# Segment sums of two graph layers: 24-bit messages as two 12-bit parts in one product of 256 columns, and half of the one-hot tiles on GpSimd

## The chip, the cores and the metric

The kernel runs on 1 core of one Trainium2 chip. The metric is the device time of one execution in microseconds (us); the time of a kernel is the median of its runs.

## The reference

Four graph layers run one after the other over 3125 nodes with 128 features, and 103125 edges (50000 random pairs in both directions and one loop per node), sorted by target. Layers 0 (attention) and 1 (softmax gathering) are not touched. The change is in layers 2 and 3. Cut to what matters:

```
# layer 2
h = concat([x[row], x[col], edge_attr]) @ W1 + b1
h = relu((h - mean) * rsqrt(var + 1e-5) * gamma + beta)     # mean, var over all edges
sums = segment_sum(h @ W2 + b2, row); counts = segment_sum(1, row)
out = x + sums / (counts + 1)
# layer 3
m = relu(concat([x[src], type_emb[edge_type]]) @ msg_W.T + msg_b)
agg = segment_sum(m, dst) / max(deg, 1)
out = layernorm(x + agg @ upd_W.T + upd_b) * g + b
```

The kernel applies the node products before the edges are formed, and W2 after the sums, so that the work per edge is: add the rows of two nodes (or of a node and a type), ReLU, add into the row of one node.

## The kernel before

Nodes lie in 25 blocks of 128 (NB = 25, KT = 50). The edges have been sorted into buckets, so that a tile of 128 edges has its sources in one block and its targets in one block. Rows are picked and summed by products with one-hot matrices. The five engines are programmed by hand: each runs its own list in order and waits on semaphores. DVE is VectorE, ACT ScalarE, PE TensorE, POOL GpSimd, SP the queue that issues the transfers.

**Layer 2** (`pe_b2_main`, `dve_b2_main`, and the loop over `main_groups()` in `act_buckets`): 325 groups of up to 4 tiles, 1225 tiles. A pass over one source block k has 13 groups and 49 tiles: a unit of 7 groups (six of 4 tiles, the last of 2) and a unit of 6 groups (five of 4, the last of 3). For each tile PE does seven bf16 products of 128 columns into a PSUM bank (lines 3472, 3474, 3476; "H" below). ACT takes the ReLU of the group's bank into `msgs` (line 3413). Then PE adds the tile into the sums of its node block by one f32 product, with the one-hot tile `col_hot` as weights and the message, with a column of ones for the count, as 129 moving columns (line 3496; "A" below). DVE makes `col_hot`, one instruction a tile (line 3279). In the last pass, k = 24, half of the tiles belong to other blocks: their product goes into bank 4 or 5 in turn (line 3493), and DVE adds the bank into `S2` and `counts` (lines 3292, 3293), before PE may use that bank again two such products later.

**Layer 3** (`pe_b3`, `dve_b3`): 319 groups, 1225 tiles. Each of the first 24 node blocks has 50 tiles in 13 groups: 7 groups of 4, then 5 of 4 and one of 2; the last block has 25 tiles in 7 groups. H is four bf16 products a tile (lines 3518, 3520), ReLU is line 3428, the one-hot tile line 3349, A is one f32 product of 128 columns (line 3533).

**Row-hots.** The weights of H are the one-hot rows of a whole unit (6 or 7 groups) in two buffers. They come by transfer as numbers, and DVE turns them into one-hots with two long instructions a unit: `dve_unit_hot` (lines 3173, 3174), placed behind the col_hots of the unit's fifth group, for the unit that follows; `dve_unit_hot3` (lines 3325, 3326) behind those of the last group but one. PE can't begin the next unit's first H without them.

**Order of PE.** H(n), A(n-1), H(n+1), A(n), ... H(n) needs the ReLU of group n-4 (four banks). DVE makes the col_hots of group n as soon as A(n-2) is done (two buffers); nothing in DVE's list waits for ACT.

Of the kernel before, what the change touches and what calls it, by code (L numbers as in the profile page):

```python
# [7 lines left out]
F32 = mybir.dt.float32  # L8
I32 = mybir.dt.int32
# [5 lines left out]
P = 128  # L15
# [285 lines left out]
class BucketSignals:  # L301


    def __init__(self, g):
# [56 lines left out]
        self.d_pair_count = self.d_window  # L361
        self.drawn_pe = self.pre_pe
# [20 lines left out]
def program(nc, a, out):  # L383
    ctx = ExitStack()
    with ctx:
# [86 lines left out]

        arena_c = sb("arena_c", [P, C_WORDS])
# [199 lines left out]
        msgs = [words(C_, 12100 + s * 516, [P, 4, D + 1]) for s in range(2)]  # L673
        col_hot = [words(C_, 13132 + s * 512, [P, 4, P]) for s in range(2)]
# [2531 lines left out]
        def dve_b2_stats(e, own):  # L3206
# [51 lines left out]
            for s in range(2):  # L3258
                e.memset(msgs[s][:, :, D:D + 1], 1.0)
# [8 lines left out]

        def dve_b2_main(e, own):
            all_groups = main_groups()  # L3270
            counts = stat[:, 2, :]
            extras = 0
            for at in range(GROUPS + 2):
                if at < GROUPS:
                    u, k, bs = all_groups[at]
                    if at >= 2:
                        e.wait_ge(sig.added_pe, at - 1)
                    for i, (b, j) in enumerate(pair_tiles(bs)):
                        hot = e.tensor_scalar(col_hot[at % 2][:, i, :], iota_row, src_lo[:, b, 2 * k + j:2 * k + j + 1], None, ALU.is_equal)  # L3279
                    hot.then_inc(sig.col_hot, 1)  # L3280
                    if at == pairs_before(u) + 4 and u + 1 < 2 * NB:
                        dve_unit_hot(e, u + 1)
                if at >= 2:
                    u, k, bs = all_groups[at - 2]
                    if k == NB - 1:
                        for b in bs:
                            if b < NB - 1:
# [4 lines left out]
                                e.tensor_tensor(S2[:, b, :], S2[:, b, :], ps[:, 0:D], ALU.add)  # L3292
                                e.tensor_tensor(counts[:, b:b + 1], counts[:, b:b + 1], ps[:, D:D + 1], ALU.add).then_inc(sig.extra_dve, 1)
                    if at - 2 == (k + 1) * NPAIR - 1:
                        ps = bank[6 + k % 2]
                        e.wait_ge(sig.added_pe, at - 1)
                        e.tensor_copy(counts[:, k:k + 1], ps[:, D:D + 1])
                        e.tensor_copy(S2[:, k, :], ps[:, 0:D]).then_inc(sig.block_dve, 1)
# [29 lines left out]
        def dve_b3(e, own):  # L3328
# [13 lines left out]
            for u in range(2 * NB + 1):  # L3342
                if u < 2 * NB:
                    b = u // 2
                    for i, ts in enumerate(unit3_tiles(u)):
                        if at >= 2:
                            e.wait_ge(sig.added3_pe, at - 1)
                        for i_, t in enumerate(ts):
                            hot = e.tensor_scalar(col_hot[at % 2][:, i_, :], iota_row, dst_lo[:, b, t:t + 1], None, ALU.is_equal)  # L3349
# [4 lines left out]
                        if i == 2 and u % 2 == 0 and u:  # L3354
                            dve_b3_block(e, b - 1)
            dve_b3_block(e, NB - 1)
# [40 lines left out]
        def act_buckets(e):  # L3397
# [274 lines left out]
```

## Time and profile before

| | before |
|---|---|
| median of 3 runs | 4507.58 us (4504.23 to 4513.55) |
| the profiled execution's own time | 4506.15 us |
| its span, first to last instruction | 4504.0 us |
| granted TensorE clock, mean over the span | 0.896 |
| busy share: PE, PE weight load, DVE, ACT, POOL | 79%, 69%, 71%, 48%, 21% |
| main loop of layer 2 | 3037.4 to 3812.4 us |
| main loop of layer 3 | 3883.5 to 4450.8 us |

Between the span and the time of the same execution lie 2.15 us. POOL's 21% lies wholly in the first half of the span; in the two loops it does nothing. A matmul's duration in the rows holds the time until its result is written, so rows overlap: the pace of PE is read from one start to the next. A f32 product stands as two records.

### The profile page before, as it was taken

How to read it: one execution, taken by the hardware profiler on the slowest of the kernel's cores; microseconds unless marked ns; L12 is line 12 of the kernel's file. 1: busy time of each engine (PE TensorE's matmuls, PEld its weight loads, DVE VectorE, ACT ScalarE, POOL GpSimd, SP SyncE). 2: the span in 40 equal slices, each digit the busy share in tenths (PEclk: the TensorE clock that was granted, in tenths of full speed). 3: DMA queues.
4: the chain of work that ended last, by engine and by line, in shares of the span. 5: the costliest groups of instructions: out<-in, count | busy, mean ns of one | idle time of the engine just before them, and what ended most of it. 6: DMA issues, size and time to landing. Idle time of an engine off the chain costs nothing.

```text
span 4504.0 us, 93109 instructions
## 1 busy us (share of the span) xinstructions
PE 3567.1 (79%) x35307; PEld 3108.5 (69%) x35307; DVE 3209.6 (71%) x7198; ACT 2176.5 (48%) x6143; POOL 964.7 (21%) x1005
## 2 busy tenths in 40 slices
PE   1488899889999451666648888669999999699996
PEld 1266666666666331666647887449999998699995
DVE  5589888878898446999868787674444445666666
ACT  2366666667777223788747667212222222333332
POOL 0466577757677400000000000000000000000000
PEclk7799998999999675878779999889999999899998
DMA  5666676767777301000011011333334432233322
GB/s 110 200 186 184 172 205 197 195 171 211 209 214 211 90 5 39 10 12 12 9 35 46 38 45 45 106 109 104 113 109 116 116 109 77 63 102 102 98 97 65
DMA packets 418314, 488.81 MB, mean 109 GB/s; under 512 B 178078, under 2 KB 329924, under 8 KB 417725
## 3 DMA queue, kind: packets, MB, share of 16 engines
q1 hardware_dynamic: 358861, 305.18, 23.7%
q0 software_dynamic: 58992, 177.50, 13.7%
q8 instruction: 288, 4.72, 0.4%
q14 instruction: 173, 1.42, 0.1%
HBM read 376.80 MB, written 105.72 MB: 107 GB/s over the span
## 4 chain that ended last, share of the span: by engine, by line
PE 62%; DVE 22%; ACT 5%; issue 4%; DMA 3%; SPq 2%; POOL 1%; DVEq 0%; POOLq 0%; ACTq 0%
PE bank L3533 6%; PE bank L3496 6%; PE bank L3520 5%; PE bank L3474 5%; PE bank L3476 5%; PE bank L2325 4%; PE bank L2331 3%; PE bank L2336 3%; PE bank L3442 2%; PE bank L2898 2%; PE bank L2316 2%; ACT arena_c L2861 2%; PE bank L2389 2%; PE bank L2307 2%; DVE arena_b L1749 2%
## 5 line engine op out<-in xcount | busy, mean ns | idle before, releaser
L1112 POOL DMA_INDIRECT arena_a<-src_table,src_tix x808 | 775.9, 960 | 353.1 <-issue 228.3
L3279 DVE TENSOR_SCALAR arena_c<-arena_c 128x128 f32<-128x128 f32 x1225 | 268.9, 281 | 402.4 <-PE bank L3496 402.4
L3413 ACT ACTIVATE arena_c<-bank 128x512 f32<-128x512 f32 (+2 forms) x325 | 186.5, 574 | 591.2 <-PE bank L3476 591.2
L2898 PE MATMUL bank<-arena_a,arena_c 128*128 128x150 f32 x1800 | 289.3, 331 | 173.4 <-ACT arena_c L2864 173.4
L3349 DVE TENSOR_SCALAR arena_c<-arena_c 128x128 f32<-128x128 f32 x1225 | 265.7, 280 | 203.6 <-PE bank L3533 203.6
L3474 PE MATMUL bank<-arena_c,arena_a 128*128 128x128 bf16 x3675 | 406.2, 219 | 0.0
L3476 PE MATMUL bank<-arena_c,arena_a 128*128 128x128 bf16 x3675 | 406.2, 219 | 0.0
L2898 PEld LDWEIGHTS bank<-arena_a,arena_c 128*128 128x128 f32 x1800 | 283.7, 225 | 176.5 <-ACT arena_c L2864 176.5
L3428 ACT ACTIVATE arena_c<-bank 128x512 f32<-128x512 f32 (+1 forms) x319 | 185.2, 581 | 386.8 <-PE bank L3520 386.8
L3533 PE MATMUL bank<-arena_c 128*128 128x128 f32 x2450 | 343.1, 282 | 0.0
L3496 PE MATMUL bank<-arena_c 128*128 128x129 f32 x2402 | 338.6, 281 | 0.0
L3520 PE MATMUL bank<-arena_c,arena_a 128*128 128x128 bf16 x3675 | 309.3, 220 | 0.0
L2861 ACT ACTIVATE arena_c<-arena_c,arena_b 128x128 f32<-128x128 f32 x900 | 265.7, 387 | 89.9 <-DVE arena_b L2778 89.9
L2331 PEld LDWEIGHTS bank<-arena_b 128*128 128x128 f32 x1616 | 224.4, 201 | 111.1 <-issue 107.5
L3533 PEld LDWEIGHTS bank<-arena_c 128*128 128x128 f32 x2450 | 299.4, 192 | 0.0
L3472 PE MATMUL bank<-src_tix,arena_a 128*128 128x128 bf16 x1225 | 268.8, 219 | 34.5 <-DVE arena_c L3156 34.5
L3496 PEld LDWEIGHTS bank<-arena_c 128*128 128x128 f32 x2402 | 294.2, 191 | 0.0
L1300 ACT ACTIVATE arena_a<-arena_a 128x128 f32<-128x128 f32 x808 | 239.3, 297 | 95.7 <-DVE arena_a L1769 88.2
L3518 PE MATMUL bank<-src_tix,arena_a 128*128 128x128 bf16 x1225 | 269.2, 220 | 15.8 <-DVE arena_a L3326 15.8
L3474 PEld LDWEIGHTS bank<-arena_c,arena_a 128*128 128x128 bf16 x3675 | 257.5, 98 | 4.0
L3520 PEld LDWEIGHTS bank<-arena_c,arena_a 128*128 128x128 bf16 x3675 | 257.8, 98 | 3.5
L3476 PEld LDWEIGHTS bank<-arena_c,arena_a 128*128 128x128 bf16 x3675 | 257.6, 98 | 0.0
(583 smaller groups left out, 9263.7 us busy)
## 6 DMA issues: line engine op xcount, KB each, us to landing
y_rows<-arena_c SPq DMA_DIRECT2D x101, 576.0 KB
arena_a<-bucket_rows SPq DMA_DIRECT2D x50, 832.0 KB
arena_a<-bucket_rows SPq DMA_DIRECT2D x50, 768.0 KB
arena_a<-bucket_lists SPq DMA_DIRECT2D x25, 896.0 KB, 4.6
pair_counts<-arena_c SPq DMA_DIRECT2D x25, 800.0 KB
arena_a<-bucket_lists SPq DMA_DIRECT2D x25, 704.0 KB, 4.4
arena_a<-src_table,src_tix POOLq DMA_INDIRECT x808
arena_c<-edge_attr SPq DMA_DIRECT2D x100, 128.0 KB
```

Source lines behind the costliest of these rows:

```text
L1112: e.indirect_dma_start(out_, None, table, bass.IndirectOffsetOnAxis(ap=idx, axis=0)).then_inc(sem, 16)
L2331: q_ = e.matmul(bank[1][:, t * P:(t + 1) * P], pick[s][:, 4 * hf + t, :], win[r][:, 0:D], start=True, stop=True)
L2861: away = e.activation(hot_pos[s][:, j, :], iota_row, ACT.Abs, bias=minus_pos[s][:, j:j + 1])
L2898: put = e.matmul(bank[2 + s][:, 0:3 * KT], hot_pos[s][:, j, :], routed_v[s][:, j, :, :].rearrange("p f k -> p (f k)"), start=(j == 0), sto ...
L3279: hot = e.tensor_scalar(col_hot[at % 2][:, i, :], iota_row, src_lo[:, b, 2 * k + j:2 * k + j + 1], None, ALU.is_equal)
L3472: e.matmul(to, attr_rows[s][:, c_], Wc12, start=True, stop=False)
L3474: e.matmul(to, row_hot[0][s][:, c_], A3[:, part, sb_ * D:(sb_ + 1) * D], start=False, stop=False)
L3476: put = e.matmul(to, row_hot[1][s][:, c_], B3[:, part, b * D:(b + 1) * D], start=False, stop=(part == 2))
L3496: put = e.matmul(bank[6 + k % 2][:, 0:D + 1], col_hot[at % 2][:, i, :], msgs[at % 2][:, i, :], start=(first and i == into_k[0]), stop=(las ...
L3518: e.matmul(to, row_hot[1][s][:, c_], E48, start=True, stop=False)
L3520: put = e.matmul(to, row_hot[0][s][:, c_], A3[:, part, k * D:(k + 1) * D], start=False, stop=(part == 2))
L3533: put = e.matmul(bank[6 + b % 2][:, 0:D], col_hot[at % 2][:, i_, :], msgs[at % 2][:, i_, 0:D], start=(first and i_ == 0), stop=(last and i ...
```

## The change

In both loops the message is made in two parts of 12 bits, in a format that PE takes as float32r: ACT writes the high part, max(x, 0) rounded, and DVE writes the low part, max(x, 0) minus the high part, with a new instruction a group that reads the PSUM bank (`dve_low_parts`). A multiplies the one-hot tile, float32r too, with both parts side by side, 256 columns a tile, and the two halves of the sum are added when a block is done (one reduction instead of a copy in layer 2; one more instruction in layer 3). Counts are no longer summed by PE: they are taken once from `node_sums`. Messages and one-hots have three buffers (RING_M = 3) instead of two. GpSimd makes the one-hots of a group's third and fourth tile (`pool_b2_main`, `pool_b3`), DVE those of the first and second. PE's order becomes H(n), A(n-2). H(n) now waits for the low part of group n-4.

```diff
+        msg_parts = part_buffers("msg_parts", base_b, 0, RING_M, [P, 2, 4, D])
+        msg_parts3 = part_buffers("msg_parts3", base_c, 7304, RING_M, [P, 2, 4, D])
+        node_hot = part_buffers("node_hot", base_a, 10752, RING_M, [P, 4, P])
...
+        def dve_low_parts(e, at, nt, high_made, low_made, parts):
+            e.wait_ge(high_made, at + 1)
+            to = parts[at % RING_M]
+            e.scalar_tensor_tensor(out=to[:, 1, 0:nt, :], in0=bank[at % 4][:, 0:nt * P].rearrange("p (t f) -> p t f", f=P), scalar=0.0,
+                                   in1=to[:, 0, 0:nt, :], op0=ALU.max, op1=ALU.subtract).then_inc(low_made, 1)
...
+        def pool_b2_main(e):
+            for at, (u, k, bs) in enumerate(main_groups()):
+                nt = len(pair_tiles(bs))
+                if nt > 2:
+                    if at >= RING_M:
+                        e.wait_ge(sig.added_pe, at - RING_M + 1)
+                    for i in range(2, nt):
+                        hot = source_hot(e, at, i)
+                    hot.then_inc(sig.col_hot_pool, 1)
...
         def dve_b2_main(e, own):
-            for at in range(GROUPS + 2):
+            for at in range(GROUPS + 3):
                 if at < GROUPS:
                     u, k, bs = all_groups[at]
-                    if at >= 2:
-                        e.wait_ge(sig.added_pe, at - 1)
-                    for i, (b, j) in enumerate(pair_tiles(bs)):
-                        hot = e.tensor_scalar(col_hot[at % 2][:, i, :], iota_row, src_lo[...], None, ALU.is_equal)
+                    dve_low_parts(e, at, nt, sig.relu, sig.low, msg_parts)
+                    if at >= RING_M:
+                        e.wait_ge(sig.added_pe, at - RING_M + 1)
+                    for i in range(min(nt, 2)):
+                        hot = source_hot(e, at, i)
                     hot.then_inc(sig.col_hot, 1)
                     if at == pairs_before(u) + 4 and u + 1 < 2 * NB:
                         dve_unit_hot(e, u + 1)
-                if at >= 2:
-                    u, k, bs = all_groups[at - 2]
+                if at >= 3:
+                    u, k, bs = all_groups[at - 3]
...
-                                e.tensor_tensor(S2[:, b, :], S2[:, b, :], ps[:, 0:D], ALU.add)
-                                e.tensor_tensor(counts[:, b:b + 1], counts[:, b:b + 1], ps[:, D:D + 1], ALU.add).then_inc(sig.extra_dve, 1)
+                                own.step(e.tensor_tensor(S2[:, b, :], S2[:, b, :], ps[:, 0:D], ALU.add))
+                                e.tensor_tensor(S2[:, b, :], S2[:, b, :], ps[:, D:2 * D], ALU.add).then_inc(sig.extra_dve, 1)
...
         def pe_b2_main(e):
-            for n in range(GROUPS + 1):
+            for n in range(GROUPS + 2):
...
-                        e.wait_ge(sig.relu, n - 3)
+                        e.wait_ge(sig.low, NB + n - 3)
...
-                if n >= 1:
-                    at = n - 1
+                if n >= 2:
+                    at = n - 2
...
-                        put = e.matmul(bank[6 + k % 2][:, 0:D + 1], col_hot[at % 2][:, i, :], msgs[at % 2][:, i, :],
+                        put = e.matmul(bank[6 + k % 2][:, 0:2 * D], hots[:, i, :], parts[:, :, i, :],
```

Layer 3 is changed in the same way (`dve_b3`, `pe_b3`, `pool_b3`). Three places in the lists of the engines:

DVE in layer 3, around the row-hots that are made in an odd unit, before (line 3349 the col_hots, 24 being six groups, 3325 and 3326 the row-hots of the next unit, 3362 the end of a block):

```order
L3349 TENSOR_SCALAR arena_c<-arena_c 128x128 x24
L3325 TENSOR_SCALAR arena_a<-arena_a,arena_c 48x3584
L3326 TENSOR_SCALAR arena_a<-arena_a,node_id 128x3584
L3349 TENSOR_SCALAR arena_c<-arena_c 128x128 x14
L3362 TENSOR_SCALAR arena_b<-bank6,stat 128x128
```

and the same place now (bank numbers kept; line 3328 the low part, 3023 the one-hots, 3386 and 3387 the row-hots):

```order
L3328 SCALAR_TENSOR_TENSOR msg_parts32_54<-bank2,msg_parts32_54 128x512
L3023 TENSOR_SCALAR node_hot2_57<-arena_c 128x128 x2
L3328 SCALAR_TENSOR_TENSOR msg_parts30_52<-bank3,msg_parts30_52 128x512
L3023 TENSOR_SCALAR node_hot0_55<-arena_c 128x128 x2
L3386 TENSOR_SCALAR arena_a<-arena_a,arena_c 48x3584
L3387 TENSOR_SCALAR arena_a<-arena_a,node_id 128x3584
L3328 SCALAR_TENSOR_TENSOR msg_parts31_53<-bank0,msg_parts31_53 128x256
```

The row-hots stand behind the same group as before, but that group now begins with an instruction that reads its bank after H and the ReLU.

DVE in the last pass of layer 2, before (line 3279 the col_hots of group n, 3292 and 3293 the additions for group n-2):

```order
L3279 TENSOR_SCALAR arena_c<-arena_c 128x128 x4
L3292 TENSOR_TENSOR arena_b<-arena_b,bank4 128x128
L3293 TENSOR_TENSOR stat<-stat,bank4 128x1
L3292 TENSOR_TENSOR arena_b<-arena_b,bank5 128x128
L3293 TENSOR_TENSOR stat<-stat,bank5 128x1
```

and now (3328 and 3310 the low part and one-hots of group n, 3355 and 3356 the additions for group n-3):

```order
L3328 SCALAR_TENSOR_TENSOR msg_parts0_49<-bank3,msg_parts0_49 128x512
L3310 TENSOR_SCALAR node_hot0_55<-arena_c 128x128 x2
L3355 TENSOR_TENSOR arena_b<-arena_b,bank4 128x128
L3356 TENSOR_TENSOR arena_b<-arena_b,bank4 128x128
L3355 TENSOR_TENSOR arena_b<-arena_b,bank5 128x128
L3356 TENSOR_TENSOR arena_b<-arena_b,bank5 128x128
```

The additions that free banks 4 and 5 now stand behind a low part as well.

PE in the last pass of layer 2, now: the last tile of H(n) (lines 3536, 3538, 3540), then A(n-2), whose first two products (3561) need the banks that those additions free, then H(n+1):

```order
L3536 MATMUL bank3<-src_tix,arena_a 128x128
L3538 MATMUL bank3<-arena_c,arena_a 128x128 x3
L3540 MATMUL bank3<-arena_c,arena_a 128x128 x3
L3561 MATMUL bank4<-msg_parts1_50,node_hot1_56 128x256
L3561 MATMUL bank5<-msg_parts1_50,node_hot1_56 128x256
L3564 MATMUL bank6<-msg_parts1_50,node_hot1_56 128x256 x2
L3536 MATMUL bank0<-src_tix,arena_a 128x128
```

Before, A(n-1) stood there, with the same four products of 129 columns.

## Rows read from the trace of the kernel before

**Rows 1.** The two loops: length, busy (xcount) PE, PEld, DVE, ACT, POOL, clock, DMA.

```profile
3037.40:3812.40 775.00, 773.20 (x11025) 768.68 (x11025) 371.83 (x1419) 186.45 (x325) 0.00 (x0) 1.00 0.38 108
3883.50:4450.80 567.30, 567.26 (x7350) 562.58 (x7350) 361.88 (x1347) 185.24 (x319) 0.00 (x0) 1.00 0.30 97
```

**Rows 2.** Timeline of a group of layer 2: start, length, instructions merged, idle before.

```profile
3400.56 1.11 PE L3496 MATMUL bank<-arena_c 128*128 128x129 f32 x8
3400.76 0.60 ACT L3413 ACTIVATE arena_c<-bank 128x512 f32<-128x512 f32 x1 [1.92 <-PE bank L3476]
3401.51 0.22 PE L3472 MATMUL bank<-src_tix,arena_a 128*128 128x128 bf16 x1
...
3401.71 0.87 DVE L3279 TENSOR_SCALAR arena_c<-arena_c 128x128 f32<-128x128 f32 x4 [1.64 <-PE bank L3496]
```

**Rows 3.** Timeline of layer 3 around two pairs of row-hots, DVE.

```profile
4113.62 1.14 DVE L3325 TENSOR_SCALAR arena_a<-arena_a,arena_c 48x3584 bf16<-48x3584 bf16 x1
4114.69 1.14 DVE L3326 TENSOR_SCALAR arena_a<-arena_a,node_id 128x3584 bf16<-128x3584 bf16 x1
...
4126.50 0.94 DVE L3326 TENSOR_SCALAR arena_a<-arena_a,node_id 128x2816 bf16<-128x2816 bf16 x1
...
4136.68 1.14 DVE L3325 TENSOR_SCALAR arena_a<-arena_a,arena_c 48x3584 bf16<-48x3584 bf16 x1
```

**Rows 4.** The same stretch, PE: the first H behind those row-hots.

```profile
4115.88 0.23 PE L3518 MATMUL bank<-src_tix,arena_a 128*128 128x128 bf16 x1
```

**Rows 5.** Timeline of layer 2, DVE: the first of a pair of row-hots.

```profile
3312.56 1.08 DVE L3173 TENSOR_SCALAR arena_a<-arena_a,node_id 128x3328 bf16<-128x3328 bf16 x1
```

**Rows 6.** Timeline of layer 2's last pass, PE and DVE.

```profile
3805.80 0.66 PE L3493 MATMUL bank<-arena_c 128*128 128x129 f32 x4
...
3807.73 0.28 DVE L3292 TENSOR_TENSOR arena_b<-arena_b,bank 128x128 f32<-128x128 f32 x1
...
3808.31 0.66 PE L3493 MATMUL bank<-arena_c 128*128 128x129 f32 x4
```

**Rows 7.** Groups of instructions: count | busy us, mean ns | idle before.

```profile
L3474 PE MATMUL bank<-arena_c,arena_a 128*128 128x128 bf16 x3675 | 406.2, 219 | 0.0
L3442 PE MATMUL bank<-arena_c,arena_a 128*128 128x384 bf16 x325 | 56.8, 334 | 13.5 <-DVE arena_c L3156 13.5
L3037 DVE SCALAR_TENSOR_TENSOR arena_c<-arena_c 128x512 f32<-128x512 f32 x150 | 102.7, 685 | 47.2 <-ACT arena_c L3082 47.0
L1087 POOL TENSOR_SCALAR_AFFINE_SELECT ident<-ident 128x128 f32<-128x128 f32 x1 | 0.3, 290 | 1.5 <-DVE edge_ok L1565 1.5
L1112 POOL DMA_INDIRECT arena_a<-src_table,src_tix x808 | 775.9, 960 | 353.1 <-issue 228.3 <-DVE arena_c L1757 124.8
```

**Rows 8.** One line's instructions: durations in ns, min/median/max, first and last start.

```profile
L1717 DVE TENSOR_SCALAR arena_b<-arena_b,node_id x25: 277/280/493, 540.8 to 857.1; 128x128 f32<-128x128 f32 x25
```

**Rows 9.** Layer 1: waits of PE on L3014, two stretches (us, times, longest).

```profile
PE bank L3114 <- DVE arena_b L3014: 3.4, 3, 1.1
PE bank L3114 <- DVE Hn L3014: 2.2, 2, 1.1
...
PE bank L3114 <- DVE Hn L3014: 5.6, 5, 1.1
PE bank L3114 <- DVE arena_b L3014: 5.6, 5, 1.1
```

**Rows 10.** Busy time and clock of those two stretches, and slices behind one wait.

```profile
2350.00:2450.00 100.00, 83.01 (x1313) 78.59 (x1311) 84.75 (x163) 74.50 (x222) 0.00 (x0) 1.00 0.11 43
2500.00:2700.00 200.00, 168.12 (x2475) 159.80 (x2474) 159.24 (x307) 138.72 (x408) 0.00 (x0) 0.92 0.11 43
...
2512.00:2513.00 1.00, 0.24 (x5) 0.24 (x6) 1.00 (x2) 0.00 (x0) 0.00 (x0) 0.93 1.01 422
2513.00:2514.00 1.00, 1.00 (x19) 1.00 (x17) 0.90 (x6) 0.00 (x0) 0.00 (x0) 0.50 0.55 218
...
2516.00:2517.00 1.00, 1.00 (x16) 0.99 (x16) 0.73 (x3) 0.76 (x4) 0.00 (x0) 0.86 0.00 0
```

More of the change, by code:

```diff
@@ L8 @@
 F32 = mybir.dt.float32
+F32R = mybir.dt.float32r
 I32 = mybir.dt.int32
@@ L361, in __init__ @@
         self.d_pair_count = self.d_window
+        self.low = self.routed
+        self.low3 = self.weighed
+        self.col_hot_pool = self.spread
+        self.col_hot3_pool = self.away
         self.drawn_pe = self.pre_pe
@@ L446, in program @@
         RING = 4
+        base_a = nc.sbuf_base
         arena_a = sb("arena_a", [P, RING * TPB * 3 * D])
+        base_b = nc.sbuf_base
         arena_b = sb("arena_b", [P, 2 * NB * D])
@@ L3000, in pool_buckets, with target_hot, pool_b3 @@
             e.wait_ge(g.nodes_ready, 4)
+            pool_b2_main(e)
+            pool_b3(e)
+        def target_hot(e, at, i, b, t):
+            return e.tensor_scalar(node_hot[at % RING_M][:, i, :], iota_row, dst_lo[:, b, t:t + 1], None, ALU.is_equal)
+        def pool_b3(e):
+            e.wait_ge(sig.split_dve, 8)
+            at = 0
+            for u in range(2 * NB):
+                for ts in unit3_tiles(u):
+                    if len(ts) > 2:
+                        if at >= RING_M:
+                            e.wait_ge(sig.added3_pe, at - RING_M + 1)
+                        for i in range(2, len(ts)):
+                            hot = target_hot(e, at, i, u // 2, ts[i])
+                        hot.then_inc(sig.col_hot3_pool, 1)
+                    at += 1
         def dve_b_hot(e, b, i):
@@ L3257, in dve_b2_stats @@
             dve_wc_parts(e, own)
-            for s in range(2):
-                e.memset(msgs[s][:, :, D:D + 1], 1.0)
+            own.step(e.tensor_copy(stat[:, 2, :], node_sums[:, 0:NB, 2]))
             dve_split(e, scaled_tables, 2)
@@ L3345, in dve_b3 @@
                     for i, ts in enumerate(unit3_tiles(u)):
[L3346 to L3349, printed above, removed]
+                        dve_low_parts(e, at, len(ts), sig.relu3, sig.low3, msg_parts3)
+                        if at >= RING_M:
+                            e.wait_ge(sig.added3_pe, at - RING_M + 1)
+                        for i_, t in enumerate(ts[0:2]):
+                            hot = target_hot(e, at, i_, b, t)
                         hot.then_inc(sig.col_hot3, 1)
@@ L3353, in dve_b3, with dve_b3_block @@
                             dve_unit_hot3(e, u + 1)
-                        if i == 2 and u % 2 == 0 and u:
-                            dve_b3_block(e, b - 1)
-            dve_b3_block(e, NB - 1)
+                        if i == 3 and u % 2 == 0 and u:
+                            dve_b3_block(e, own, b - 1)
+            dve_b3_block(e, own, NB - 1)
             e.wait_ge(sig.block3_dve, NB)
             e.drain().then_inc(g.nodes_ready, 1)
-        def dve_b3_block(e, b):
+        def dve_b3_block(e, own, b):
             e.wait_ge(sig.added3_pe, groups3_before(2 * b + 2))
-            e.tensor_scalar(S1[:, b, :], bank[6 + b % 2][:, 0:D], stat[:, 0, b:b + 1], None, ALU.mult).then_inc(sig.block3_dve, 1)
+            own.step(e.tensor_reduce(S1[:, b, :], bank[6 + b % 2][:, 0:2 * D].rearrange("p (a f) -> p f a", a=2), AX, ALU.add))
+            e.tensor_scalar(S1[:, b, :], S1[:, b, :], stat[:, 0, b:b + 1], None, ALU.mult).then_inc(sig.block3_dve, 1)
         def dve_split_y(e):
@@ L3504, in pe_b3 @@
             flat = [(u, i, ts) for u in range(2 * NB) for i, ts in enumerate(unit3_tiles(u))]
-            for n in range(len(flat) + 1):
+            by_pool = 0
+            for n in range(len(flat) + 2):
                 if n < len(flat):
```

60 lines of the change are left out of this document (37 added, 23 removed).

## The prediction

> **What bounds the kernel now.** I read the busy time of the two loops first, then the timeline of one group, then the places where DVE does its long instructions. In both loops PE is busy to within 2 us of 775.0 and of 567.3 us at the full clock, while DVE is busy 371.8 and 361.9, ACT 186 and 185, and POOL does nothing [rows 1]. Whatever is saved of PE there is saved of the whole, as long as nobody makes PE wait. In a group of layer 2, A takes from 3400.56 to the next H at 3401.51, 0.95 us for 8 records, so 0.118 a record and 0.236 a tile [rows 2]; a whole group is 3808.31 - 3805.80 = 2.51 us [rows 6], which leaves 1.56 for the 28 products of H, 0.056 each. A pass of layer 2 is 49 x (7 x 0.056 + 0.236) = 30.8 us, and 25 of them make 770 of the 775. In layer 3 a block lasts 4136.68 - 4113.62 = 23.06 us [rows 3], and 50 x (4 x 0.056 + 0.236) = 23.0. So both loops go at PE's pace.
>
> How far DVE runs ahead is what the reader should see next. Its col_hots start at 3401.71, when A has ended, in the middle of H(n) [rows 2]: they don't wait for H or ReLU. Even so, in layer 3 the second row-hot ends at 4114.69 + 1.14 = 4115.83 [rows 3], and PE begins the next unit's H at 4115.88 [rows 4]. That cover is used up to the last 0.05 us.
>
> **The change, part by part.** *A.* No float32r product is in the trace. From below, 256 more columns at bf16's pace: (334 - 219) / 256 = 0.45 ns a column [rows 7], 0.115 us a tile; from above, f32's pace for 256 columns, 0.47. One record's pace, 0.118, is what a weight load and 256 columns at 0.45 ns take side by side, and I take it: half of the 0.236 before. For its page on number formats (the Trainium skill, "FP8 and Floating Point Precision", TensorE Precision Notes: true fp32 takes four passes) one pass of twice the columns would be half too. If nothing waits, a pass becomes 49 x 0.51 = 25.0 and a block 50 x 0.342 = 17.1 us: 25 x 5.8 + 24.5 x 5.9 = 290 us off.
>
> *DVE.* The low part is new: a two-operand instruction of 512 columns takes 0.685 us [rows 7], and I let the next start 0.61 behind it (rows overlap by 0.07: 1.14 long, 1.07 apart, [rows 3]). Two one-hots are 0.39 ((0.87 - 0.28) / 3 = 0.197 apart, [rows 2]). So 1.0 us a group for 0.8 before, with the row-hots 17 us a block in layer 3: DVE's total fits under PE. Its order doesn't. The row-hots now stand behind a low part that waits for H and ReLU. From the end of H's issue, at time 0: ReLU 0.20 to 0.80 (3400.56 to 3400.76, 0.60 long, [rows 2]), low part 0.84, one-hots 1.45, row-hots from 1.85. In layer 3's odd units they end at 1.85 + 1.07 + 1.14 = 4.06, and PE may begin at 4.10. It has until then only A(n-2) 0.47, the H of 2 tiles 0.45 and another A 0.47: 1.39. **It stands 2.7 us.** In even units (0.94 long, [rows 3]): 1.85 + 0.87 + 0.94 + 0.05 = 3.7 against 0.47 + 0.90 + 0.47 = 1.84: **1.9 us.** Layer 2's odd units (1.08 long, [rows 5]): 1.85 + 1.01 + 1.08 + 0.05 = 4.0 against 0.47 + 1.17 + 0.47 = 2.1: **1.9 us**; its even units have one more group in between, 3.8, and stand 0.1.
>
> *GpSimd.* Nothing of this form is in the trace. Its 128x128 select took 0.29 us, the longest common instruction 0.96 [rows 7]; I take 0.35, near the select, so 0.7 a group, under every period. They begin when A is done. One pair falls between A(n-2) and DVE's one-hots and meets nothing; the pair behind A(n-1) falls into the row-hots. A DVE instruction of the one-hots' form took 0.277 at its shortest, but 0.493 once while POOL was at work [rows 8]. So I add one POOL instruction, 0.35, to each pair of row-hots. The bounds are 0 (they never meet) and about 1.0 (both get in between, at 0.5 each); 0.96 for one is the far end. The Trainium skill ("SBUF — State Buffer", Who interferes with whom) says that a two-port DVE instruction and a GpSimd one exclude each other for their whole length, whichever came first. By that rule 0.35 or 0.7 is right; the stretched row above agrees with it but doesn't prove it.
>
> *Last pass of layer 2.* Banks 4 and 5 are freed by additions that now wait for the low part of the group whose H has just ended. After the two one-hots at 1.85: an addition 0.28 [rows 6] and, behind a semaphore, a second; bank 4 is free at 2.5, bank 5 at 3.0. PE then does A's last three products, 0.36, and H, 1.56: 4.9 us a group instead of 2.5. Ten such groups, the short ones (3 and 4 us), the first (2.0) and a pair of row-hots (1.9) make 60 us for 30.8.
>
> *Clock.* In layer 1 PE waits 1.1 us on L3014: five times between 2350 and 2450, with the clock at full, and ten times between 2500 and 2700, with a mean clock of 0.92 [rows 9, 10]. The slices behind one wait show it: 0.93, three at 0.50, then 0.86, which is 1.7 us lost [rows 10]; ten of these are the 0.08 x 200 = 16 us missing. So 10 of 15 waits of 1.1 us had a fall to 1.2 GHz behind them. PE was not densely at work around those, and here it is, so for waits of 2.2 us I take a fall after 6 in 10, for 3.1 us after 8 in 10 (bounds none and all), each 1.7 us. In the last pass PE works 2.0 of 4.9 us; at the lower level a group would be H 3.1, the chain 2.9 and the last three products 0.7, so 6.7; I take 75 us for the pass (bounds 60, 80).
>
> *Sum.* Layer 2, 24 passes: 25.0 + 1.9 + 0.1 + 2 x 0.35 = 27.6, and 1.0 for the clock: 28.6 for 30.8, 24 x 2.2 = **-53**. Last pass 75 - 31 = **+44**. Layer 3: 17.1 + 1.9 + 2.7 + 0.7 = 22.4, and 1.4 falls, 2.4: 24.8 for 23.06, 24 x 1.7 = **+41**. The ends of the loops, where a low part now lies between the last ReLU and the last A: **+2**. Together +34 on 4506.15, the profiled execution's time, which lies 1.4 us under the median: **4540 us**. The counts, their column and the memsets cost and give nothing: they lay beside PE. The reduction per block lies on DVE behind A's that it has already waited for, and costs nothing while DVE keeps 0.3 us a group; without that, 0.7 a block.
>
> **The rivals.** *The clock stays up.* The standing times remain, the falls don't: 24 x (27.6 - 30.8) = -77, last pass +29, layer 3 24 x (22.4 - 23.06) = -17, ends +2: 4443 us, faster. It decides the sign; the ten waits with falls speak against it, the five without for it. *No collision between POOL and DVE*, with falls: 0.7 off each pass and block: 4506, no change. *POOL is dearer* (0.5 us or more, or both its instructions get in between): another 0.7 a pass and block and a few more falls: 4585; at 0.96 each layer 3 would be bound by POOL at 24 x 0.96 = 23.0 a block before any wait, some 4620. *PE never waits*, because the row-hots are ready after all: 4216; the order of DVE's list speaks against it. *float32r goes at f32's pace*: 0.47 a tile adds 0.23 x 2450, over 5000 us.
>
> **How the numbers follow.** Forecast 0.40, clock up 0.22, no collision 0.13, POOL dearer 0.15, PE never waits 0.05, f32's pace 0.03, other 0.02. The range 4440 to 4605 takes in the first four. 0.2% (9 us) is about what a measurement of this kernel can tell from no change. Faster by more: 0.22 + 0.05 + 0.05 of "no collision" + 0.04 of the forecast's lower edge = 0.36; within: 0.08; slower: 0.56. The forecast's own range is 4500 to 4580.
>
> **What the profile would show.** A: records of 128x256, 0.118 apart. DVE's low part at 0.68, behind ReLU. PE idle before the first H of a unit, put down to the row-hots, once a pass in layer 2 and twice a block in layer 3, 1.9 to 3 us: some 65 us in layer 2 and 125 in layer 3. In the last pass ten waits on the additions, 2.5 us each and more. POOL's one-hots at 0.35, and row-hots up to 0.35 longer or later than 1.14. The granted clock 0.9 in layer 3 instead of 1.00, half to two thirds in the last pass. Most likely to be wrong: the number of falls, and POOL's price.

## The result, and the profile after

The changed kernel takes **4491.89 us** (median of 20 runs) and the kernel before 4508.16 (median of 20). The ratio is 0.9964, with a 95% interval of 0.9954 to 0.9974: 0.36% faster, where 0.7% slower was forecast. One of the changed kernel's runs, at 4855.59 us and a mean clock of 0.71 instead of 0.88, is left out of the comparison. The profiled execution took 4497.49 us.

The first part of the page, of the changed kernel:

```profile
PE 3385.2 (75%) x32857; PEld 2891.7 (64%) x32857; DVE 3410.4 (76%) x6679; ACT 2176.8 (48%) x6143; POOL 1770.1 (39%) x2167
```

Busy time and clock of the 24 passes of layer 2, its last pass, and the loop of layer 3, in the columns of [rows 1]:

```profile
3045.90:3713.00 667.10, 629.73 (x9470) 612.23 (x9471) 444.30 (x1058) 180.14 (x314) 359.35 (x557) 1.00 0.44 125
3713.00:3780.40 67.40, 42.43 (x334) 37.40 (x331) 26.39 (x86) 6.32 (x12) 11.19 (x19) 0.62 0.02 5
3852.40:4441.90 589.50, 489.07 (x6125) 466.23 (x6125) 462.88 (x1103) 185.27 (x319) 438.24 (x587) 0.92 0.29 93
```

Layer 2 goes from 775.0 to 734.5 us (-40.5) and layer 3 from 567.3 to 589.5 (+22.2) [rows 1]. Between the loops lie 72.0 us instead of 71.1. The loop of layer 2 begins 8.5 us later than before, though ahead of it only a copy of the counts stands in place of the memsets, and PE's wait just ahead of the loop is 34.5 us in both; in the experiments, whose code up to there is the same, it begins between 3036 and 3051, so this is the spread of a single execution. PE is no longer busy throughout: 94% in the first stretch, 63% and 83% in the others.

PE's waits in the two loops (us in total, times, longest):

```profile
PE bank L3587 <- DVE arena_a L3387: 115.7, 50, 15.9
PE bank L3536 <- DVE arena_a L3211: 37.4, 24, 1.6
...
PE bank L3561 <- DVE arena_b L3356: 24.8, 10, 4.3
```

The first two are the waits for the row-hots (3387 in layer 3, where the longest one is the wait ahead of the loop, and 3211 in layer 2), the third is that for the additions in the last pass. They stand where the prediction put them.

A unit's end in layer 2 (timeline; it answers to [rows 2, 5]):

```profile
3401.44 0.72 PE L3564 MATMUL bank<-msg_parts,node_hot 128*128 128x256 f32 x4
3401.67 0.60 ACT L3476 ACTIVATE msg_parts<-bank 128x512 fp32r<-128x512 f32 x1 [1.50 <-PE bank L3540]
3402.00 0.23 PE L3536 MATMUL bank<-src_tix,arena_a 128*128 128x128 bf16 x1
...
3402.30 0.69 DVE L3328 SCALAR_TENSOR_TENSOR msg_parts<-bank,msg_parts 128x512 fp32r<-128x512 f32 x1 [0.89 <-ACT msg_parts L3476]
...
3402.91 0.47 DVE L3310 TENSOR_SCALAR node_hot<-arena_c 128x128 fp32r<-128x128 f32 x2
...
3403.30 1.08 DVE L3210 TENSOR_SCALAR arena_a<-arena_a,node_id 128x3328 bf16<-128x3328 bf16 x1
...
3403.97 2.45 POOL L3310 TENSOR_SCALAR node_hot<-arena_c 128x128 fp32r<-128x128 f32 x2 [1.11 <-PE bank L3564]
3404.29 1.08 DVE L3211 TENSOR_SCALAR arena_a<-arena_a,node_id 128x3328 bf16<-128x3328 bf16 x1
...
3405.43 0.23 PE L3536 MATMUL bank<-src_tix,arena_a 128*128 128x128 bf16 x1 [1.56 <-DVE arena_a L3211]
...
3432.99 0.23 PE L3536 MATMUL bank<-src_tix,arena_a 128*128 128x128 bf16 x1 [1.56 <-DVE arena_a L3211]
```

H's issue ends at 3401.44, where A begins; then come ReLU, low part, one-hots, two row-hots, and the next unit's H at 3405.43. These are 3.99 us, 4.0 in the prediction. The row-hots are 1.08 long, as before, and nothing lies between them. The same wait comes back 27.56 us later: that is a pass (30.8 before). Four products of A take 3402.00 - 3401.44 = 0.56 us, 0.14 a tile. From H's issue to the next PE has 0.56 + 1.16 (three tiles of H) + 0.56 = 2.3 us of work, so it stands 1.7; the profile, which counts idle time from the end of the last record, has 1.56.

The same place in layer 3 (timeline), and the clock around it (two windows):

```profile
4110.83 0.72 PE L3605 MATMUL bank<-msg_parts,node_hot 128*128 128x256 f32 x4
...
4112.62 2.65 POOL L3023 TENSOR_SCALAR node_hot<-arena_c 128x128 fp32r<-128x128 f32 x1 [1.24 <-PE bank L3605]
...
4112.68 1.14 DVE L3386 TENSOR_SCALAR arena_a<-arena_a,arena_c 48x3584 bf16<-48x3584 bf16 x1
4113.74 1.14 DVE L3387 TENSOR_SCALAR arena_a<-arena_a,node_id 128x3584 bf16<-128x3584 bf16 x1
...
4114.94 0.23 PE L3587 MATMUL bank<-src_tix,arena_a 128*128 128x128 bf16 x1 [2.41 <-DVE arena_a L3387]
...
4128.16 0.23 PE L3587 MATMUL bank<-src_tix,arena_a 128*128 128x128 bf16 x1 [1.66 <-DVE arena_a L3387]
...
4138.89 0.23 PE L3587 MATMUL bank<-src_tix,arena_a 128*128 128x128 bf16 x1 [2.41 <-DVE arena_a L3387]
```

```profile
4114.90:4118.90 4.00, 3.96 (x37) 3.87 (x37) 1.81 (x6) 0.60 (x1) 2.31 (x4) 0.57 0.25 80
4118.90:4136.00 17.10, 15.44 (x215) 14.81 (x213) 14.23 (x35) 6.59 (x12) 13.34 (x20) 1.00 0.23 75
```

From the end of H's issue (4110.83) to the next H (4114.94) are 4.11 us. A block is 4138.89 - 4114.94 = 23.95 us (23.06 before). It holds a wait of 2.41 us, one of 1.66, and one fall to the lower level, behind the longer wait: 4.00 us at 0.57, so 1.7 us lost. Slices of 1 us over the whole loop show 24 such falls, one behind each wait of 2.41 us, and a low clock at the loop's start and end: 44 us lost in all, which is the 0.92 of the loop.

### The profile page after: what moved, and what is told of

Its sections match the earlier page's. It is cut to its first block, busy times and chain, and to the rows that moved or that the text cites. A ratio compares the mean times of both kernels' runs of the same rounds, so it can differ in the third digit from the quotient of the medians.

```text
span 4495.7 us, 88908 instructions
## 1 busy us (share of the span) xinstructions
PE 3385.2 (75%) x32857; PEld 2891.7 (64%) x32857; DVE 3410.4 (76%) x6679; ACT 2176.8 (48%) x6143; POOL 1770.1 (39%) x2167
## 4 chain that ended last, share of the span: by engine, by line
PE 55%; DVE 27%; ACT 7%; issue 4%; DMA 3%; SPq 2%; POOL 1%; DVEq 0%; POOLq 0%; ACTq 0%
PE bank L3589 5%; PE bank L3540 4%; PE bank L3538 4%; PE bank L2342 4%; PE bank L2348 3%; PE bank L2353 3%; PE bank L3564 3%; PE bank L3605 3%; PE bank L2915 3%; ACT arena_c L2878 2%; PE bank L3505 2%; PE bank L2333 2%; PE bank L3587 2%; PE bank L3536 2%; DVE arena_b L1766 2%
## 5 line engine op out<-in xcount | busy, mean ns | idle before, releaser
L3310 POOL TENSOR_SCALAR node_hot<-arena_c 128x128 fp32r<-128x128 f32 x575 | 370.5, 656 | 1650.7 <-DVE arena_c L3193 1294.1
L3328 DVE SCALAR_TENSOR_TENSOR msg_parts<-bank,msg_parts 128x512 fp32r<-128x512 f32 (+2 forms) x644 | 426.4, 662 | 387.7 <-ACT msg_parts L3476 262.4
L3023 POOL TENSOR_SCALAR node_hot<-arena_c 128x128 fp32r<-128x128 f32 x587 | 440.4, 762 | 225.7 <-PE bank L3605 148.5
L3476 ACT ACTIVATE msg_parts<-bank 128x512 fp32r<-128x512 f32 (+2 forms) x325 | 186.5, 574 | 546.9 <-PE bank L3540 546.9
L3538 PE MATMUL bank<-arena_c,arena_a 128*128 128x128 bf16 x3675 | 412.5, 222 | 0.0
L3540 PE MATMUL bank<-arena_c,arena_a 128*128 128x128 bf16 x3675 | 412.1, 222 | 0.0
L3491 ACT ACTIVATE msg_parts<-bank 128x512 fp32r<-128x512 f32 (+1 forms) x319 | 185.3, 581 | 408.4 <-PE bank L3589 408.4
L3587 PE MATMUL bank<-src_tix,arena_a 128*128 128x128 bf16 x1225 | 285.4, 233 | 115.7 <-DVE arena_a L3387 115.7
L3589 PE MATMUL bank<-arena_c,arena_a 128*128 128x128 bf16 x3675 | 336.9, 230 | 0.0
L3536 PE MATMUL bank<-src_tix,arena_a 128*128 128x128 bf16 x1225 | 275.3, 225 | 71.9 <-DVE arena_a L3211 37.4
L3589 PEld LDWEIGHTS bank<-arena_c,arena_a 128*128 128x128 bf16 x3675 | 279.3, 104 | 0.0
L3538 PEld LDWEIGHTS bank<-arena_c,arena_a 128*128 128x128 bf16 x3675 | 262.9, 100 | 0.2 <-issue 0.2
L3540 PEld LDWEIGHTS bank<-arena_c,arena_a 128*128 128x128 bf16 x3675 | 262.3, 99 | 0.0
L2342 PE MATMUL bank<-weights,arena_c 128*128 128x512 f32 x404 | 244.8, 690 | 3.1 <-DVE arena_a L1784 3.1
L1766 DVE TENSOR_SCALAR arena_b<-bank,win_node 128x512 f32<-128x512 f32 x202 | 151.6, 750 | 124.0 <-PE bank L2324 123.4
L1303 ACT ACTIVATE arena_c<-bank 128x272 f32<-128x272 f32 x404 | 157.4, 390 | 171.7 <-PE bank L2334 171.1
```

The costliest lines, as they stand in the source:

```text
L2342: e.matmul(bank[0][:, :], eat[s][:, hf, :], Wt4[:, :], start=True, stop=True).then_inc(g.addend_pe, 1)
L3023: return e.tensor_scalar(node_hot[at % RING_M][:, i, :], iota_row, dst_lo[:, b, t:t + 1], None, ALU.is_equal)
L3310: return e.tensor_scalar(node_hot[at % RING_M][:, i, :], iota_row, src_lo[:, b, 2 * k + j:2 * k + j + 1], None, ALU.is_equal)
L3328: e.scalar_tensor_tensor(out=to[:, 1, 0:nt, :], in0=bank[at % 4][:, 0:nt * P].rearrange("p (t f) -> p t f", f=P), scalar=0.0, in1=to[:, 0, ...
L3536: e.matmul(to, attr_rows[s][:, c_], Wc12, start=True, stop=False)
L3538: e.matmul(to, row_hot[0][s][:, c_], A3[:, part, sb_ * D:(sb_ + 1) * D], start=False, stop=False)
```

## The experiments

The kernel before, on the same chips, had medians of 4508.93, 4509.72 and 4510.41 us (7 runs each, 4 of each experiment); each ratio below is to it. Differences to the changed kernel carry some 2 us of doubt: so far apart lie the medians of the kernel before.

**1. The row-hots' place.** In both layers they move from behind the low part and the one-hots to directly ahead of the low part of the same group:

```diff
+                    if at == pairs_before(u) + 4 and u + 1 < 2 * NB:
+                        dve_unit_hot(e, u + 1)
                     dve_low_parts(e, at, nt, sig.relu, sig.low, msg_parts)
...
-                    if at == pairs_before(u) + 4 and u + 1 < 2 * NB:
-                        dve_unit_hot(e, u + 1)
```

> The row-hots of the next unit stand ahead of the low part of their group instead of behind it, in both layers; nothing else is changed. Theory of order (the waits of PE at the units' ends come from row-hots that stand behind an instruction that waits for H and ReLU): the wait before L3536 in layer 2, 1.6 us a pass now, goes; a pass 27.56 -> 25.8 us. In layer 3 the row-hots can begin one group earlier (1.4 us), the waits fall from 2.4 and 1.8 to about 1 and 0.5, and with them the one fall of the clock a block (1.7 us): block 23.94 -> 19.5 to 20. Together 24 x 1.8 + 24 x 4.2 = 143 us faster than the changed kernel, about 4350. Theory of the shared port (GpSimd's one-hots hold up DVE's row-hots): the place in the list doesn't matter, less than 20 us of difference.

Measured: **4360.42 us**, ratio 0.9669 (0.9653 to 0.9685). Waits and windows of this kernel:

```profile
PE bank L3587 <- DVE arena_a L3387: 52.8, 50, 15.7
...
PE bank L3561 <- DVE arena_b L3356: 23.0, 10, 2.4
```

```profile
3038.50:3661.00 622.50, 622.19 (x9407) 608.28 (x9407) 443.27 (x1050) 178.71 (x312) 371.64 (x553) 1.00 0.47 132
3661.00:3730.30 69.30, 45.78 (x397) 40.47 (x394) 29.16 (x96) 7.44 (x13) 14.10 (x23) 0.70 0.08 25
3800.40:4298.60 498.20, 456.97 (x6115) 428.60 (x6116) 450.05 (x1098) 184.69 (x318) 410.91 (x587) 1.00 0.34 110
```

The wait in layer 2 is gone and PE is busy throughout again; in layer 3 each pair of row-hots still costs (52.8 - 15.7) / 49 = 0.76 us. Layer 3 is 91 us shorter than in the changed kernel, and the clock is at 1.00: the place of the row-hots in DVE's list cost 131 us, waits and falls together.

**2. The additions' place.** In the last pass they stand ahead of the group's low part (the block under `if at >= 3` moves ahead of the one under `if at < GROUPS`).

> The additions of banks 4 and 5 into S2 (and the reduction at a pass's end) stand ahead of the low part of the group instead of behind its one-hots; nothing else. Theory of order: in the last pass of layer 2 (67.4 us now, clock 0.62 of full) the ten waits on L3356 go, the clock stays up, and the pass takes about 27 us: 40 us faster than the changed kernel, about 4452. If instead two f32r products in a row into banks 4 and 5 or the additions themselves are slow, or the low clock comes from something else than the waits: less than 15 us.

Measured: **4461.38 us**, ratio 0.9889 (0.9872 to 0.9905), 30.5 us under the changed kernel. The rest is as it was (PE's waits in layer 3 115.7 us, 50 times); in the last pass the waits for the additions fall from 24.8 us (ten) to 5.2 (seven). 30.5 us came back where 40 was expected.

**3. No one-hots on GpSimd.** DVE makes all four:

```diff
-                    for i in range(min(nt, 2)):
+                    for i in range(nt):
...
-            pool_b2_main(e)
-            pool_b3(e)
```

> All one-hots on DVE, none on GpSimd; all else as in the changed kernel. Theory of order: the waits stay and grow by two more one-hots (0.4 us) in the chain: pass 27.56 -> 28.3, block 23.94 -> 24.7, or 26.4 if a second fall of the clock comes in; 40 to 80 us slower than the changed kernel, 4530 to 4575. DVE's one-hots are 0.28 again instead of 0.32. Theory of the shared port: with GpSimd silent the waits of PE shrink, pass 25.5 to 26.5, at least 25 us faster than the changed kernel.

Measured: **4577.4 us**, ratio 1.0145 (1.0128 to 1.0162). Its waits of PE for the row-hots (lines 3385 and 3209 here), then the second row-hot's durations in this kernel, and in the changed one:

```profile
PE bank L3582 <- DVE arena_a L3385: 139.1, 50, 15.7
PE bank L3534 <- DVE arena_a L3209: 46.8, 24, 2.0
```

```profile
L3385 DVE TENSOR_SCALAR arena_a<-arena_a,node_id x50: 934/1040/1141, 3886.5 to 4515.5; 128x3584 bf16<-128x3584 bf16 x25, 128x2816 bf16<-128x2816 bf16 x25
```

```profile
L3387 DVE TENSOR_SCALAR arena_a<-arena_a,node_id x50: 934/1038/1141, 3851.1 to 4433.7; 128x3584 bf16<-128x3584 bf16 x25, 128x2816 bf16<-128x2816 bf16 x25
```

PE stands as before, and 0.4 us longer each time, with GpSimd idle: 46.8 / 24 = 1.95 us for 1.56 in layer 2, and (139.1 - 15.7) / 49 = 2.5 for 2.0 in the mean of layer 3. That is what two more one-hots in the chain were expected to cost. The waits are DVE's order, and not its quarrel with GpSimd; and the row-hots take the same 1.04 us with and without GpSimd at work. DVE's one-hots do lose something: their median is 0.315 us beside GpSimd's and 0.278 with GpSimd idle. GpSimd's half is worth 85.5 us (4577.4 - 4491.9): 33 us are the longer waits and some 36 a lower clock behind them (0.97 in layer 2, 0.90 in layer 3).

**4. Row-hots one group earlier still, and the additions first.** As 1 and 2, but `+ 4` becomes `+ 3` (and `- 2` becomes `- 3` in layer 3).

> Row-hots ahead of the low part of the group before theirs (one group earlier than in the first of these kernels), and the additions first. Theory of order: no wait of PE at a unit's end, in both layers. Pass 25.6, last pass 27, block bound by DVE: 13 groups of 1.0 to 1.1, row-hots 3.9, end of block 0.8, so 18 to 19 us, clock 1.00. 24 x 2.0 + 40 + 24 x 5 = 208 us faster than the changed kernel, about 4285. Rival: the lists of the next unit haven't landed that early (about 6 us behind their issue), DVE waits for them, and a block stays at 20 to 22.

Measured: **4360.74 us**, ratio 0.967 (0.9654 to 0.9686): a miss by 76 us, and no better than the first kernel. What PE waits for here, and then what DVE waits for:

```profile
PE bank L3605 <- DVE node_hot L3023: 60.6, 51, 1.6
...
PE bank L3564 <- DVE msg_parts L3328: 20.9, 23, 1.6
```

```profile
DVE arena_a L3210 <- DMA arena_a<-bucket_rows: 48.2, 37, 2.4
```

The waits for the row-hots are gone, and others have come. In layer 2 DVE now stands 1.3 us before a pair of row-hots for its transfer, and the low part queued behind it is late for A; in layer 3, where only one such wait for a transfer is left (0.3 us), it is A that waits for DVE's one-hots, which now stand behind the row-hots. Beside experiment 5, which differs in this alone, layer 2 takes 26 us more and layer 3 13. A place in a list has an early edge as well as a late one.

**5. Row-hots ahead of the same group's low part, and the additions first.** As 1 and 2 together.

> Row-hots directly ahead of the low part of the same group in both layers, and in the last pass of layer 2 the additions ahead of the low part. Theory (both are places in DVE's order, and they lie in different stretches): the saving of the row-hots moved alone (131 us against the changed kernel) and of the additions moved alone (30 us) add up: about 4330 us. Rival (the two share a cover, or the order of the additions makes the row-hots late again, as a two-groups-ahead version gave no more than the row-hots alone): 4355 us or more. In the profile a pass of layer 2 at 25.9, the last pass at about 37, a block of layer 3 at 20.3.

Measured: **4327.58 us**, ratio 0.9592 (0.9575 to 0.9608). 131.5 + 30.5 = 162 us was expected and 164 came: they add up.

**6. One-hots ahead of the low part.** Only these two change places, from the fourth group on:

```diff
-                    dve_low_parts(e, at, nt, sig.relu, sig.low, msg_parts)
...
                     hot.then_inc(sig.col_hot, 1)
+                    dve_low_parts(e, at, nt, sig.relu, sig.low, msg_parts)
```

> Only DVE's two one-hots and the low part of each group change places; the row-hots stay behind both. They need only that a product three groups back is done, so they should run while DVE waits for the ReLU. Theory: the chain from the end of a unit's last-but-one H to the next H gets shorter by the two one-hots, 0.5 us: PE's waits for the row-hots fall from 1.56 to about 1.0 in layer 2 and from 1.6 and 2.4 to about 1.1 and 1.9 in layer 3: 0.5 a pass and 1.0 a block, 24 x 1.5 = 36 us, and some 6 us in the last pass: 4450 us. If the clock falls only behind waits of over 2 us, the fall in each block (1.7 us) goes too: 4410 us. Rival (the one-hots of a group are held up by PE's products, so that the low part comes later): no gain, 4490 or more.

Measured: **4442.55 us**, ratio 0.9848 (0.9832 to 0.9865), between the two values of the theory. The waits (row-hots at 3390 and 3211 here):

```profile
PE bank L3593 <- DVE arena_a L3390: 96.3, 50, 15.7
...
PE bank L3542 <- DVE arena_a L3211: 28.0, 24, 1.2
```

A wait in layer 2 falls from 1.56 to 28.0 / 24 = 1.17 us, those in layer 3 from 2.0 to (96.3 - 15.7) / 49 = 1.6 us in the mean: 0.4 each, for the 0.5 expected. In layer 3 they are 2.02 and 1.27 in turn, and the fall of the clock goes with only some of the longer ones: the slices show 14 falls for the 24 of the changed kernel.

**7. Only layer 3's odd units.** The change of experiment 1 in layer 3 alone, and there for odd u alone (`if i == UNIT3_GROUPS[u] - 2 and u % 2 == 1 and u + 1 < 2 * NB`).

> Only the row-hots made in layer 3's odd units stand directly ahead of the low part; everything else is as in the changed kernel. This takes away PE's wait of 2.4 us and leaves the one of 1.6 in the even units. Theory (the clock falls behind the wait of 2.4 and not behind waits of 1.6): the one fall in each block goes with it, so a block goes from 23.94 to 20.3 to 20.5, where DVE's own work bounds it: 24 x 3.5 = 84 us off, 4408 us. Rival (the fall belongs to the sum of standing time in a block and comes behind the other wait instead): 22.0 a block, 4445 us, with one stretch of half clock in each block as before.

Measured: **4425.49 us**, ratio 0.9806 (0.9789 to 0.9822). Layer 3 in it, and its waits:

```profile
3849.70:4372.00 522.30, 453.00 (x6115) 428.29 (x6116) 458.90 (x1098) 184.86 (x318) 409.17 (x587) 1.00 0.32 105
```

```profile
PE bank L3589 <- DVE arena_a L3387: 83.5, 50, 15.9
...
PE bank L3538 <- DVE arena_a L3211: 37.4, 24, 1.6
```

The wait of 2.41 us is now one of 1.07, the other is 1.66 as before, and the clock is at 1.00 instead of 0.92: no fall is left behind either, and none has moved to the wait that stayed. The block takes 522.3 / 24.5 = 21.3 us, where I had said 20.3 to 20.5: I had taken DVE's work as the bound and had not added up the waits that stay, (83.5 - 15.9) / 24 = 2.8 us a block for 1.55 in the first kernel.

**8. The high part alone.** This kernel leaves the low part out of the sums; the low part itself is still made. The product is of 128 columns:

```diff
-                        put = e.matmul(bank[6 + k % 2][:, 0:2 * D], hots[:, i, :], parts[:, :, i, :],
+                        put = e.matmul(bank[6 + k % 2][:, 0:D], hots[:, i, :], parts[:, 0, i, :],
```

> The low part is still made, but the product takes only the high part, 128 columns, and nothing adds the low half; one addition instead of two per extra tile. It prices the 256 columns. Theory (a product's time goes by its columns, 0.14 us for 256): 0.07 us a tile for 128 columns. In layer 2 the cover of the row-hots shrinks too, 0.07 x 9 tiles, so a pass falls from 27.56 by 49 x 0.07 - 0.6 = 2.8 to about 24.8; a block of layer 3, bounded by DVE and by the waits, by about 2 to 22: 24 x 4.8 = 115 us, and some 10 in the last pass: about 4370 us. Rival (the product is bound by the load of its float32r weights, not by its columns): a tile of A stays at 0.14, the pass at 27 and more, 4480 us.

Measured: **4477.77 us**, ratio 0.9928 (0.9911 to 0.9944). Four tiles of A and the H behind them (timeline), then the weight loads of A in the passes of layer 2 (grouped, mean ns behind the comma); last, those of H in the changed kernel:

```profile
3401.60 0.64 PE L3563 MATMUL bank<-msg_parts,node_hot 128*128 128x128 f32 x4
3402.08 0.23 PE L3535 MATMUL bank<-src_tix,arena_a 128*128 128x128 bf16 x1
```

```profile
L3563 PEld LDWEIGHTS bank<-msg_parts,node_hot 128*128 128x128 f32 x1162 | 156.7, 194 | 0.0
```

```profile
L3538 PEld LDWEIGHTS bank<-arena_c,arena_a 128*128 128x128 bf16 x3474 | 243.2, 98 | 0.2 <-issue 0.2
```

Half of the columns takes 0.48 us for four tiles, 0.12 a tile, for the 0.14 of 256 columns. The rival was right: columns hardly count. The 0.02 are 49 us over 2450 tiles, of which only 14 arrive, because the cover of the row-hots shrinks too: PE's waits for them grow (41.0 us for 37.4 in layer 2, 122.1 for 115.7 in layer 3), and the clock falls (0.98 and 0.89 for 1.00 and 0.92). Before, a record with 129 f32 columns took 0.119 us [rows 2]. What the three have in common is a load of 128 weights of four bytes, 190 ns long, twice a bf16 one. That it is this load which sets 0.12 is my reading; the runs show only that going from 256 columns to 128 takes off no more than 0.02. The load's record is itself longer than the 0.12 from one product to the next, so loads overlap, and 190 ns is not a price to add up. The Trainium skill ("TensorE: Matmul & The Clock Gate", Weight-path perf modes) keeps its fast weight load for inputs that are not FP32; this trace agrees as far as float32r loads take the time of the f32 ones and not that of the bf16 ones, but no run shows which kind of load was used.

**9. All three moves.** Experiment 5 and experiment 6 in one kernel.

> The three moves together: row-hots first, additions first, and in each group the one-hots ahead of the low part. With the first two alone PE still waits 0.77 us for each pair of row-hots in layer 3 (52.8 less the first wait of 15.7, over 48), a block takes 20.34 us and PE's own work in it is 17.9 to 18.3. Theory (what is left is the low part's place behind the row-hots, which the one-hots lengthen): 0.5 us less per pair, a block at 19.4 and no change in layer 2, whose passes are at PE's pace already (25.85): 24 x 0.95 = 23 us off 4327.6, so about 4305. Rival (DVE's total work, 18.2 us busy in 20.34, is what bounds the block together with its waits for the ReLU, wherever the one-hots stand): 4320 or more.

Measured: **4299.61 us**, ratio 0.9531 (0.9509 to 0.9554). Its passes, last pass and layer 3, and its waits in layer 3:

```profile
3050.90:3672.00 621.10, 621.09 (x9398) 607.64 (x9399) 444.67 (x1051) 178.23 (x311) 386.27 (x552) 1.00 0.45 132
3672.00:3705.40 33.40, 30.20 (x404) 27.32 (x402) 28.90 (x95) 7.94 (x14) 14.62 (x24) 1.00 0.19 51
3777.40:4258.40 481.00, 456.62 (x6115) 430.72 (x6116) 441.67 (x1099) 184.66 (x318) 467.78 (x587) 0.99 0.35 114
```

```profile
PE bank L3593 <- DVE arena_a L3390: 37.8, 26, 15.9
```

This version is 4.7% faster than the kernel before and 192 us under the changed one, with the same arithmetic as the latter. What it gains over the changed kernel is the order of DVE's list alone. PE is busy throughout the 24 passes and 95% of layer 3. (The profiled execution, at 4316.03 us, was the longest of the four.)

## Why the prediction was wrong

The sign was wrong: 0.7% slower was forecast, 0.4% faster was measured. The miss is 48 us of 4508 (4540 for 4492), inside the range. The sum said +34 on the profiled execution, which came out at -8.7, or -17 without the 8.5 us at the head. Two terms of the sum failed, the POOL instruction added to each pair of row-hots (34 us over both loops) and the falls of the clock (41 us). Step by step:

- **The chain behind ReLU: right.** 4.0 us in layer 2 and 4.10 in layer 3 were forecast from H's end to the next H; 3.99 and 4.11 were measured. The low part (0.69) and the next start 0.61 behind it are as said.
- **A at 0.118 a tile: too low.** It is 0.14: 49 x 0.022 = +1.1 us a pass and a block. Part of it came back, since the same A's are the cover of the row-hots: PE stood 1.56 us by the profile where 1.9 + 0.1 was forecast, 2.41 and 1.66 where 2.7 and 1.9 was. In all +0.7 a pass and +0.6 a block.
- **"So I add one POOL instruction, 0.35, to each pair of row-hots": failed.** GpSimd's one-hot costs 0.60, not 0.35, and still adds nothing to the row-hots: it is GpSimd that stands. In the timeline of layer 3 its one-hot begins 0.06 us ahead of the first row-hot and takes 2.65 us, until both are done, while they keep their 1.14. Experiment 3 shows the same from the other side. 0.7 off each pass and block, 17 us in each loop. The Trainium skill ("SBUF — State Buffer", Who interferes with whom) says that issue order decides who blocks. The trace agrees as far as one side stands for the whole of the other's instruction, and a one-hot of DVE was still running when GpSimd's began; but GpSimd's also stood through the second row-hot, which began 1.12 us after it, and why it didn't come in between the two is not shown. What GpSimd loses there is covered: the only wait of A for a one-hot in the two loops is one of 0.7 us, and for one of DVE's.
- **"for waits of 2.2 us I take a fall after 6 in 10, for 3.1 us after 8 in 10": failed for layer 2.** The 24 waits of 1.56 us had no fall: the clock is at 1.00 over 667 us. In layer 3 there is one fall a block for the 1.4 forecast, 1.7 us each as forecast. 1.0 off each pass, 0.7 off each block.
- **Last pass: right in kind, 67.4 us for 75.** Ten waits of 2.5 us, the clock at 0.62. Experiment 2 gets 30.5 us back by moving the additions.

The pass was forecast at 28.6 and is 27.56, the block at 24.8 and is 23.95: 24 x (-1.04), -8 for the last pass and 24 x (-0.85) make -53 on +34, so -19, beside the -17 measured. The rival that came true is *the clock stays up* for layer 2, and *no collision* for both. That 4492 lies as near to 4540 as it does is partly luck: the two failed terms and the last pass are 83 us too many, and some 30 us that A cost more hide a part of them.

The two failed terms are not independent. The share of falls was applied to waits of 2.2 us (1.9 and the POOL instruction), and the waits that came were 1.56; in layer 3 those forecast at 2.2 came at 1.66, without a fall, and those forecast at 3.1 at 2.41, with one each. Where waits of about the forecast length did come, so did falls (windows of layer 2 in experiment 3, of layer 3 in experiment 6, of layer 2 in experiment 8):

```profile
3045.00:3741.00 696.00, 647.00 (x9401) 625.09 (x9401) 527.68 (x1603) 178.74 (x312) 0.00 (x0) 0.97 0.41 118
3828.80:4379.00 550.20, 469.67 (x6105) 447.37 (x6105) 463.73 (x1099) 184.41 (x318) 448.74 (x586) 0.95 0.31 100
3036.10:3690.00 653.90, 614.01 (x9392) 608.26 (x9393) 423.57 (x1048) 178.14 (x311) 363.38 (x552) 0.98 0.43 126
```

Slices of 1 us show how many: 11 falls behind 24 waits of 1.95 us, 14 behind 24 of 2.02 us, 6 behind 24 of 1.71 us. So 6 in 10 for 2.2 us was no bad share; it was the length of the wait, and with it the collision, that was wrong. Nor is the share a property of the length alone. In layer 3 of experiment 8 two waits of the same length, 25 us apart, were followed by different clocks (timeline, then the windows behind each):

```profile
3945.60 0.29 PE L3586 MATMUL bank<-src_tix,arena_a 128*128 128x128 bf16 x1 [2.59 <-DVE arena_a L3386]
...
3970.17 0.23 PE L3586 MATMUL bank<-src_tix,arena_a 128*128 128x128 bf16 x1 [2.59 <-DVE arena_a L3386]
```

```profile
3945.00:3951.00 6.00, 5.40 (x45) 5.41 (x46) 2.68 (x8) 1.19 (x2) 2.93 (x5) 0.50 0.26 88
3970.00:3978.00 8.00, 7.83 (x118) 7.83 (x118) 6.47 (x20) 3.13 (x6) 6.53 (x12) 1.00 0.16 53
```

The source of the share, layer 1, had it too: "10 of 15" should be 9 of 15 (the slices of [rows 10]'s second stretch show nine falls, 15.4 us lost), and the waits between 2350 and 2450 had none while the next twelve in a row had one each. What sets off a fall stays open. Whether PE's denser work (83% busy in [rows 10], and busy between the waits here) is what spared the waits of 1.56 us was not tested.

So where did the gain go that PE's own work promises? With no wait for row-hots a pass takes 622 / 24 = 25.9 us, for 30.8 before. A block takes 481 / 24.5 = 19.6 in the last version, for 23.06, and still holds some 0.9 us of waits; the 17.1 of the prediction was never reached. The changed kernel gives 37 + 100 us of it to waits for the row-hots, some 41 to falls in layer 3, and 34 to the last pass. By stage the last version is 46 us shorter in the 24 passes, 34 in the last pass and 108 in layer 3, 188 of the 192.

## What to carry to other kernels

When an engine's work is made to wait for something new, look at what is queued behind it in the same list, and put ahead of it all that doesn't depend on it: here the order of three kinds of instruction on DVE was worth 192 us, twelve times the change itself. Move it only as far as its data has landed and nothing more urgent comes to stand behind it: one group too early cost 33 us. And a price that hangs on another estimate (the falls of the clock on the length of the waits) goes when that one goes; where the two decide the sign, give the case without them as much chance.

## What the runs showed of the hardware

- A product with four-byte weights took 0.12 us a record with 128 float32r columns (experiment 8) and with 129 f32 ones (the kernel before), and 0.14 with 256 float32r columns (the changed kernel); loads of such weights took 190 to 194 ns, of bf16 ones 98.
- A 128x128 is_equal on GpSimd with float32r output took 0.60 us; DVE's took 0.28 with GpSimd idle and 0.315 beside it (medians). GpSimd's that met DVE's row-hots took up to 1.79 us in layer 2 and 2.65 in layer 3, and DVE's row-hots no longer than before.
- Falls of the granted clock to the lower of its two levels, behind PE's waits for row-hots: none of 24 at 1.56 us, 11 of 24 at 1.95 us (experiment 3, layer 2), 14 of 24 at 2.02 us (experiment 6, layer 3), all 24 at 2.41 us; none with 1.66 us and 1.07 in turn (experiment 7). The length doesn't decide alone: 6 of 24 at 1.71 us (experiment 8, layer 2), and in its layer 3 waits of 2.59 us with and without one.
